# A graph network on one core: the compares of the source histogram cut into quarters

## The chip, the cores and the metric

The kernel runs on one core of a Trainium2 chip. The metric is the device time of one execution in microseconds (us). Three runs of the kernel before gave 4375.13, 4377.79 and 4395.61 us, a median of 4377.79 us.

## The reference

The reference computes two layers of a graph network over 12,500 nodes with 32 features and 212,500 edges (`src`, `dst`, sorted by `dst`). Cut to what matters here:

```python
h = relu(layernorm(x))
deg_out = segment_sum(ones, src); deg_in = segment_sum(ones, dst)
agg = segment_sum((h * rsqrt(max(deg_out, 1)))[src], dst)         # layer 1
x = x + relu((agg * rsqrt(max(deg_in, 1))) @ weight + bias)
h = relu(layernorm(x))
m = messages(h[src], edge_attr_4, relu(edge_attr_32 @ W1 + b1) @ W2 + b2)   # layer 2
x = x + segment_sum(m, dst) + skip(h)
```

`deg_out` is a histogram: how often each node stands in `src`.

## The kernel before, in words

The edges are cut into 208 chunks of 1024 (`CHUNKS`), a chunk into 8 tiles of 128 edges. Four chunks form a ring (`RING`): four buffers of the tile `g` hold the rows gathered for four chunks. The gather is on GpSimd (`POOL`, L352): one indirect DMA per tile of 128 edges, 8 to a chunk. It reads the row numbers in `idx`, which SyncE (`SP`) loads for each chunk after the gather that last used the slot has landed (`load1`, L286).

GpSimd's order is fixed. It first gathers rows of the input `x_rows` for the first 32 chunks (`EARLY`, 256 gathers, into a kept copy), since the normalised table isn't there yet. Then it waits for `table1_out` and gathers the 176 other chunks of layer 1 from `table1` (1408 gathers), then it waits for `table2_out` and gathers all 208 chunks of layer 2 from `table2` (1664 gathers).

`table1` needs the histogram of `src`, and the histogram is the part that the change touches. A node's number is split into two digits, `dig_p` (128 values, the partition) and `dig_r` (100 values, the row in it, `NR`), both bf16. For 16 tiles of 128 edges at a time (`HB` = 16, a batch; 104 batches in all, `HBATCH`), VectorE compares a constant with each digit, L749: one `is_equal` of 128 x 16 = 2048 elements a partition into `oh_p`, one of 100 x 16 = 1600 elements into `oh_r`. Both outputs and the constants are bf16. The second compare increments `hist_ready`. TensorE (L506 to L508) waits for it, multiplies the 16 one-hot pairs of the batch (`oh_p` as weights, `oh_r` as moving data, 100 columns) into one PSUM bank, and the last of the 16 increments `hist_used`. `oh_p` and `oh_r` have two buffers: before batch n VectorE waits until batch n - 2 was used (`wait(dve, hist_used, n - 1)`). After the last batch VectorE makes `norm_src` from the counts (L761 to L763) and the table `hn` (L764), and ScalarE's queue writes `table1` (L411). VectorE then goes on with the range of `dst` of every chunk (L769, L770), which SyncE writes out and reads back as `bound` (L298, L301) before it goes on with the `idx` of the first chunks that are gathered from `table1` (the second loop of `load1`).

Then VectorE clears the sums (L773, a memset) and starts on the segment sums of layer 1.

Of the kernel before, what the change touches and what calls it, by code (L numbers as in the profile page):

```python
# [26 lines left out]
ALU = mybir.AluOpType  # L27
# [6 lines left out]
P = 128  # L34
# [23 lines left out]
EPS = 1e-5  # L58
ALPHA, C110, SI_SCALE = 0.25, 1.0 / np.sqrt(3.0), 1.0 / np.sqrt(float(MUL))
HB = 16  # L60
HBATCH = CHUNKS * TILES // HB
EARLY_LINKS = 6
MID_LINKS = 24
# [3 lines left out]
def gnn_program(nc, x_rows, src_all, src_chunks, src_rows, dst_all, dst_chunks, edge_t, sh_chunks,  # L67
                w_l0, b_l0, w1, b1, w2, skip_w, sel_a, sel_b, ident_in, out):
    assert EARLY % RING == 0 and REG_ITERS > A_ITERS + 1
    assert CHUNKS % (2 * HB // TILES) == 0 and CHUNKS % 2 == 0  # L70
    with ExitStack() as ctx:
# [54 lines left out]
        dig_r, o = hist[:, o:o + T_ALL], o + T_ALL  # L126
        oh_p, o = hist[:, o:o + 2 * P * HB].rearrange("p (b j t) -> p b j t", b=2, t=HB), o + 2 * P * HB
        oh_r, o = hist[:, o:o + 2 * NR * HB].rearrange("p (b j t) -> p b j t", b=2, t=HB), o + 2 * NR * HB
        zero_b, o = hist[:, o:o + P], o + P
# [3 lines left out]
        iotas = prod_a[:, :, :, :].rearrange("p b t k -> p (b t k)").bitcast(BF16)  # L133
        iota_p = iotas[:, 0:P * HB].rearrange("p (j t) -> p j t", t=HB)
        iota_r = iotas[:, P * HB:(P + NR) * HB].rearrange("p (j t) -> p j t", t=HB)

# [68 lines left out]
        def wait(eng, s, value):  # L205

            if not isinstance(value, int) or value > 0:
                eng.wait_ge(s, value)
# [287 lines left out]
        def _(pe):  # L496
# [7 lines left out]
            def count(i):  # L504
                for b in range(2):
                    pe.wait_ge(hist_ready, 2 * i + b + 1)  # L506
                    for t in range(HB):
                        mm = pe.matmul(deg, oh_p[:, b, :, t], oh_r[:, b, :, t], start=False, stop=False,  # L508
                                       skip_group_check=True)
                    mm.then_inc(hist_used, 1)  # L510

            with pe.Fori(0, HBATCH // 2) as i:
                count(i)
# [157 lines left out]
        def _(dve):  # L671
# [72 lines left out]
            def count(i):  # L744
                for b in range(2):
                    n = 2 * i + b
                    wait(dve, hist_used, n - 1)
                    for iota, dig, oh, m in ((iota_p, dig_p, oh_p, P), (iota_r, dig_r, oh_r, NR)):
                        ins = dve.tensor_tensor(oh[:, b, :, :], iota,  # L749
                                                dig[:, None, bass.ds(n * HB, HB)].to_broadcast([P, m, HB]),  # L750
                                                ALU.is_equal)
                    ins.then_inc(hist_ready, 1)

            count(0)
            with dve.Fori(1, HBATCH // 2) as i:
                count(i)
# [389 lines left out]
```

## Time and profile before

| | us |
|---|---|
| median of 3 runs | 4377.79 |
| the profiled execution | 4373.49 |
| its span | 4371.7 |
| VectorE busy | 2761.8 (63%) |
| TensorE busy | 2969.1 (68%) |
| GpSimd busy | 3306.5 (76%) |

The span is cut into three stages: the histogram with its setup up to about 349 us, layer 1 up to about 2204 us (GpSimd's wait for the second table ends there), layer 2 after that. Busy time counts only what an engine executes: the 0.3 us between two gathers is not in GpSimd's 76%.

### The profile page before, as it was taken

How to read it: one execution, taken by the hardware profiler on the slowest of the kernel's cores; microseconds unless marked ns; L12 is line 12 of the kernel's file. 1: busy time of each engine (PE TensorE's matmuls, PEld its weight loads, DVE VectorE, ACT ScalarE, POOL GpSimd, SP SyncE). 2: the span in 40 equal slices, each digit the busy share in tenths (PEclk: the TensorE clock that was granted, in tenths of full speed). 3: DMA queues.
4: the chain of work that ended last, by engine and by line, in shares of the span. 5: the costliest groups of instructions: out<-in, count | busy, mean ns of one | idle time of the engine just before them, and what ended most of it. 6: DMA issues, size and time to landing. Idle time of an engine off the chain costs nothing.

```text
span 4371.7 us, 66218 instructions
## 1 busy us (share of the span) xinstructions
PE 2969.1 (68%) x17022; PEld 2223.1 (51%) x17023; DVE 2761.8 (63%) x4668; ACT 747.0 (17%) x2428; POOL 3306.5 (76%) x3334
## 2 busy tenths in 40 slices
PE   6993444444222222222279999999999999999999
PEld 5772444434222222211256667666666666666676
DVE  7775444343222222211169998999989999999898
ACT  0000000001000000000043333333323333333232
POOL 7777777777777777777767777777777777777775
PEclk9999965555555555555589998999999999999898
DMA  2002111111011011110111111111111111111111
GB/s 51 11 11 44 37 37 42 37 37 28 15 15 15 15 15 15 15 15 14 15 27 29 28 29 28 29 27 29 28 28 29 29 28 28 29 28 28 27 29 19
DMA packets 224085, 113.80 MB, mean 26 GB/s; under 512 B 148848, under 2 KB 212145, under 8 KB 223953
## 3 DMA queue, kind: packets, MB, share of 16 engines
q0 software_dynamic: 106496, 54.74, 8.5%
q1 hardware_dynamic: 106281, 39.22, 3.9%
q10 hardware_dynamic: 11280, 19.53, 1.3%
q8 instruction: 10, 0.16, 0.0%
q14 instruction: 18, 0.15, 0.0%
HBM read 108.30 MB, written 4.92 MB: 26 GB/s over the span
## 4 chain that ended last, share of the span: by engine, by line
POOL 62%; issue 23%; PE 7%; DVE 4%; DMA 2%; ACT 1%; POOLq 1%; DVEq 1%; ACTq 0%
POOL g L352 62%; PE ps L524 3%; PE ps L626 2%; DMA g<-table,idx 2%; PE ps L576 1%; PE ps L614 1%; DVE onehot L794 0%; ACT acc_b L454 0%; DVE hn L947 0%; DVE ef L930 0%; ACT root L425 0%; DVE stat L704 0%; DVE stat L701 0%; ACT q L475 0%; PE ps L660 0%
## 5 line engine op out<-in xcount | busy, mean ns | idle before, releaser
L352 POOL DMA_INDIRECT g<-table,idx x3072 | 2995.8, 975 | 955.7 <-issue 924.9
L524 PE MATMUL ps<-onehot,g 128*33 128x68 f32 x2816 | 350.4, 317 | 989.6 <-issue 954.6
L626 PE MATMUL ps<-w_s,hid 128*128 128x256 f32 x3328 | 901.3, 418 | 2.2 <-DVE prod_a L1002 2.0
L626 PEld LDWEIGHTS ps<-w_s,hid 128*128 128x128 f32 x3328 | 645.8, 204 | 452.7 <-issue 366.5
L524 PEld LDWEIGHTS ps<-onehot,g 128*33 128x33 f32 x2816 | 307.3, 173 | 1030.0 <-issue 1004.6
L1007 DVE TENSOR_REDUCE msg_b<-prod_b 128x128 f32<-128x1024 f32 x416 | 827.7, 1990 | 0.0
L806 DVE TENSOR_TENSOR acc_a<-acc_a,ps 33x68 f32 (+1 forms) x416 | 89.9, 216 | 1111.7 <-PE ps L524 1086.4
L614 PE MATMUL ps<-ef,w_s 32*64 32x512 f32 x832 | 479.9, 658 | 6.5 <-issue 6.4
L463 ACT ACTIVATE hid<-ps,b_s 64x512 f32<-64x512 f32 x416 | 282.2, 678 | 1153.2 <-PE ps L614 1151.1
L524 PEld LDWEIGHTS ps<-onehot,prod_a 128*128 128x128 f32 x3328 | 402.8, 194 | 121.8 <-issue 114.4
L524 PE MATMUL ps<-onehot,prod_a 128*128 128x68 f32 x3328 | 410.7, 277 | 76.7 <-issue 68.6
L475 ACT ACTIVATE q<-g,sh 128x32 f32<-128x32 f32 x1664 | 374.4, 308 | 298.3 <-DMA g<-table,idx 298.0
L991 DVE TENSOR_TENSOR prod_b<-ps,q 128x768 f32<-128x768 f32 x416 | 394.3, 948 | 18.4 <-PE ps L626 18.3
L352 POOL DMA_INDIRECT g<-x_rows,idx x256 | 310.1, 1211 | 79.8 <-issue 77.7
L794 DVE TENSOR_TENSOR onehot<-iota_all,dst_rel 128x544 f32<-128x544 f32 x416 | 299.6, 720 | 61.7 <-issue 53.2
L508 PE MATMUL ps<-acc_b 128*128 128x100 bf16 x1664 | 313.6, 370 | 33.5 <-DVE acc_b L749 33.5
L508 PEld LDWEIGHTS ps<-acc_b 128*128 128x128 bf16 x1664 | 246.5, 148 | 100.4 <-DVE acc_b L749 33.6
L1002 DVE TENSOR_TENSOR prod_a<-ps,q 128x512 f32<-128x512 f32 x416 | 283.0, 680 | 0.0
L524 PE MATMUL ps<-onehot,msg_b 128*56 128x68 f32 x3328 | 250.0, 231 | 0.0
L524 PEld LDWEIGHTS ps<-onehot,msg_b 128*56 128x56 f32 x3328 | 218.4, 134 | 15.1
L425 ACT ACTIVATE root<-stat 128x4 f32<-128x4 f32 x50 | 10.3, 205 | 1092.4 <-DVEq L698 1092.4
L976 DVE TENSOR_TENSOR vsh<-g,sh 128x192 f32<-128x192 f32 x208 | 80.7, 388 | 166.0 <-ACT q L476 165.1
(111 smaller groups left out, 1936.3 us busy)
## 6 DMA issues: line engine op xcount, KB each, us to landing
g<-table,idx POOLq DMA_INDIRECT x3072
ef<-edge_t SPq DMA_DIRECT2D x208, 128.0 KB
ef<-src_rows ACTq DMA_DIRECT2D x31, 512.0 KB, 3.6
idx<-src_chunks SPq DMA_DIRECT2D x416, 4.0 KB
g<-x_rows,idx POOLq DMA_INDIRECT x256
sh<-sh_chunks SPq DMA_DIRECT2D x208, 16.0 KB
table<-hn ACTq DMA_DIRECT2D x1, 1600.0 KB, 8.4
table<-hn ACTq DMA_DIRECT2D x25, 64.0 KB, 1.6
```

The lines of the kernel that those rows point to most:

```text
L352: pool.indirect_dma_start(out=g[:, j, t, 0:FEAT], out_offset=None, in_=table, in_offset=bass.IndirectOffsetOnAxis(ap=idx[:, j, t:t + 1], a ...
L463: act.activation(hid[0:HID, h, :], ps[0:HID, H_BANK + h, :], ACT.Relu, bias=b1_s[:, 0:1]).then_inc(hidden_ready, 1)
L475: act.activation(q[:, j % 2, t, 8:40], g[:, j, t, 0:FEAT], ACT.Copy, scale=sh[:, j, t, 0:1])
L508: mm = pe.matmul(deg, oh_p[:, b, :, t], oh_r[:, b, :, t], start=False, stop=False, skip_group_check=True)
L524: mm = pe.matmul(ps[0:m, S_BANK + b, col:col + WIN], r, oh(t), start=(t == 0), stop=(t == TILES - 1))
L614: pe.matmul(ps[0:HID, H_BANK + h, :], w1_s[32 * j:32 * j + 32, :], ef[32 * j:32 * j + 32, 512 * h:512 * h + 512], start=True, stop=True, t ...
L626: mm = pe.matmul(w_ps[h][:, t, :], hid[:, h, P * t:P * t + P], w2_s[:, :], start=True, stop=True)
L794: dve.tensor_tensor(onehot[:, b, :, :], iota_all[:, None, 0:WIN].to_broadcast([P, TILES, WIN]), dst_rel[:, bass.ds(c * TILES, TILES)][:, : ...
L806: ins = dve.tensor_tensor(here, here, ps[0:m, S_BANK + b, col:col + WIN], ALU.add)
L991: dve.tensor_tensor(prod_b[:, h, :, 0:3, :].rearrange("p t m (i o) -> p t m i o", o=MUL), w[:, :, 128:192].rearrange("p t (i o) -> p t i o ...
L1002: dve.tensor_tensor(prod_a[:, b, 4 * h:4 * h + 4, :].rearrange("p t (k o) -> p t k o", o=MUL), w[:, :, 0:128].rearrange("p t (k o) -> p t ...
L1007: dve.tensor_reduce(msg_b[:, b, 4 * h:4 * h + 4, 0:32].rearrange("p t (g o) -> p t g o", o=MUL), prod_b[:, h, :, :, :].rearrange("p t g (i ...
```

## The change

Each of the two compares of a batch becomes four. The output and the constant are cut along the digit's values: four times 32 x 16 = 512 elements in place of 2048, and four times 25 x 16 = 400 in place of 1600. The digits (`dig`) are the same 16 columns for each piece. `hist_ready` is incremented by the last of the eight, and the wait for `hist_used` still stands ahead of the first. Nothing else is changed.

```diff
+PIECES = 4
 ...
                     n = 2 * i + b
                     wait(dve, hist_used, n - 1)
                     for iota, dig, oh, m in ((iota_p, dig_p, oh_p, P), (iota_r, dig_r, oh_r, NR)):
-                        ins = dve.tensor_tensor(oh[:, b, :, :], iota,
-                                                dig[:, None, bass.ds(n * HB, HB)].to_broadcast([P, m, HB]),
-                                                ALU.is_equal)
+                        for part_m in range(0, m, m // PIECES):
+                            rows_m = slice(part_m, part_m + m // PIECES)
+                            ins = dve.tensor_tensor(oh[:, b, rows_m, :], iota[:, rows_m, :],
+                                                    dig[:, None, bass.ds(n * HB, HB)].to_broadcast([P, m // PIECES, HB]),
+                                                    ALU.is_equal)
                     ins.then_inc(hist_ready, 1)
```

## Rows read from the trace of the kernel before

**Rows 1.** The page: the chain that ended last, and GpSimd's two gather groups.

```profile
POOL 62%; issue 23%; PE 7%; DVE 4%; DMA 2%; ACT 1%; POOLq 1%; DVEq 1%; ACTq 0%
...
L352 POOL DMA_INDIRECT g<-table,idx x3072 | 2995.8, 975 | 955.7 <-issue 924.9
...
L352 POOL DMA_INDIRECT g<-x_rows,idx x256 | 310.1, 1211 | 79.8 <-issue 77.7
```

**Rows 2.** The longest wait of GpSimd: us in total, times, longest.

```profile
POOL g L352 <- DMA table<-hn: 19.9, 1, 19.9
```

**Rows 3.** Line L749, the compares: duration in ns min/median/max, first and last start; then the idle time before them.

```profile
L749 DVE TENSOR_TENSOR acc_b<-prod_a,msg_b x104: 1220/1226/1230, 33.3 to 343.2; 128x2048 bf16<-128x2048 bf16 x104
...
L749 DVEq FUSED_REGOPS  x102: 65/69/82, 38.7 to 343.1; - x102
...
  PE ps L508: 90.9, 102
```

**Rows 4.** Timeline, VectorE and TensorE at the first three batches: start us, duration us.

```profile
34.45 0.98 DVE L749 TENSOR_TENSOR acc_b<-prod_a,acc_b 128x1600 bf16<-128x1600 bf16 x1
35.35 1.22 DVE L749 TENSOR_TENSOR acc_b<-prod_a,msg_b 128x2048 bf16<-128x2048 bf16 x1
35.49 0.58 PE L508 MATMUL ps<-acc_b 128*128 128x100 bf16 x2 [33.48 <-DVE acc_b L749]
38.86 1.23 DVE L749 TENSOR_TENSOR acc_b<-prod_a,msg_b 128x2048 bf16<-128x2048 bf16 x1 [1.39 <-PE ps L508]
```

**Rows 5.** Timeline 101 to 104 us, VectorE and GpSimd, one period of the histogram.

```profile
101.49 0.94 POOL L352 DMA_INDIRECT g<-x_rows,idx  x1 [0.30 <-issue]
102.17 1.23 DVE L749 TENSOR_TENSOR acc_b<-prod_a,msg_b 128x2048 bf16<-128x2048 bf16 x1 [0.90 <-PE ps L508]
102.74 1.47 POOL L352 DMA_INDIRECT g<-x_rows,idx  x1 [0.30 <-issue]
103.31 0.98 DVE L749 TENSOR_TENSOR acc_b<-prod_a,acc_b 128x1600 bf16<-128x1600 bf16 x1
```

**Rows 6.** Timeline 353 to 392 us, GpSimd and VectorE, after the histogram.

```profile
353.08 3.43 POOL L352 DMA_INDIRECT g<-x_rows,idx  x1 [0.30 <-issue]
355.61 2.28 DVE L769 TENSOR_REDUCE mm_c<-prod_b 104x2 f32<-104x2048 int32 x1
...
363.76 10.78 DVE L773 MEMSET acc_a<- 128x12868 f32 x1 [2.75 <-issue]
364.62 0.94 POOL L352 DMA_INDIRECT g<-x_rows,idx  x1 [0.30 <-issue]
365.87 0.94 POOL L352 DMA_INDIRECT g<-x_rows,idx  x1 [0.30 <-issue]
...
391.45 0.94 POOL L352 DMA_INDIRECT g<-table,idx  x1 [0.30 <-issue]
```

**Rows 7.** Timeline 355 to 373 us, the DMA queues of ScalarE and SyncE.

```profile
355.72 0.45 ACTq L411 DMA_DIRECT2D table<-hn  x1
...
366.24 6.22 SPq L286 DMA_DIRECT2D idx<-src_chunks  x2
```

**Rows 8.** DMA issues of the same stretch: KB each, median us to landing.

```profile
table<-hn ACTq DMA_DIRECT2D x1, 1600.0 KB, 8.4
bound<-bounds SPq DMA_DIRECT2D x2, 104.0 KB, 4.6
```

**Rows 9.** Timeline 2405 to 2407 us, short VectorE instructions in layer 2.

```profile
2405.26 0.94 DVE L991 TENSOR_TENSOR prod_b<-ps,q 128x768 f32<-128x768 f32 x1
2406.13 0.41 DVE L996 TENSOR_TENSOR prod_b<-ps,q 128x256 f32<-128x256 f32 x1
2406.46 0.68 DVE L1002 TENSOR_TENSOR prod_a<-ps,q 128x512 f32<-128x512 f32 x1
2407.06 1.99 DVE L1007 TENSOR_REDUCE msg_b<-prod_b 128x128 f32<-128x1024 f32 x1
```

## Prediction, made before the changed kernel was run

> **What bounds the kernel.** I read the chain of waits first. 62% of it is GpSimd's gathers and 23% is "issue", the 0.3 us between two of them [rows 1]. GpSimd has one large wait, 19.9 us for a table [rows 2]. It is the one for the second table, at the end of layer 1, because the first gather from table 1 at 391.45 us stands 0.30 us behind the gather before it, like any other [rows 6]. So the histogram isn't waited for. It could end later, up to a point, at no cost, and an earlier end brings nothing. What counts in the first 391 us is how fast GpSimd gets through its 256 gathers from the input.
>
> Those are slow: 1211 ns each against 975 ns later [rows 1]. Undisturbed, a gather takes 0.94 us and the next starts 1.25 us later (364.62, 365.87 [rows 6]). In the histogram they alternate between 0.94 and 1.47 us [rows 5]. The long ones tell why. The one at 102.74 ends at 104.21, 0.90 us after VectorE's second compare starts at 103.31 [rows 5]; the one at 353.08 ends at 356.51, 0.90 us after VectorE goes on to L769 at 355.61 [rows 6]. So about 0.05 us into a gather GpSimd needs something that a running compare holds; it gets it at the end of that one instruction, even if VectorE goes on at once, and needs 0.90 us from there. VectorE's memset of 10.78 us, under which gathers take 0.94 us [rows 6], doesn't hold it. The Trainium skill says of this (SBUF — State Buffer, "Who interferes with whom") that a VectorE instruction with two SBUF inputs contends with a GpSimd instruction that reads SBUF. The trace agrees, but not with its "whole instruction" the other way round: no compare is longer than 1230 ns, with 104 of them beside gathers [rows 3].
>
> The histogram itself is set by TensorE. From 38.86 to 343.2 us there are 101 batches, 3.01 us each, and before 102 of them VectorE waits for TensorE, 0.89 us on average [rows 3, 4]. Two gathers fit into a batch: 2 x 1.25 + 0.51 of waiting = 3.01.
>
> **The change, part by part.**
>
> *VectorE's time.* Removed: 208 compares; added: 832. What one costs beside the streaming is to be read from start to start, since a compare without a wait starts some 0.08 us before the record of the last ends: 1.14 us for 2048 elements (102.17, 103.31 [rows 5]), 0.90 for 1600 (34.45, 35.35 [rows 4]). In layer 2, 256, 512 and 768 f32 elements take 0.33, 0.60 and 0.87 us: 1.05 ns an element and 0.06 us fixed [rows 9]. Half of 1.05 ns (bf16) for 2048 and 1600 leaves 0.07 us fixed. I take 0.07, the row nearest in kind. A piece of 512 then takes 0.27 + 0.07 = 0.34, one of 400 takes 0.21 + 0.07 = 0.28, the eight 2.48 us in place of 2.04. Lower bound of the fixed part: the straight line through 1.14 and 0.90 gives 0.04 (eight: 2.3). Upper bound: the records' whole durations, no overlap, 0.16 (eight: 3.15).
>
> *Does the histogram get longer?* TensorE starts on batch 1 at 35.49 + 3.01 = 38.50 and VectorE on batch 2 at 38.86, 0.36 later. The first matmul stands 0.06 us behind the end of the last compare (35.43 [rows 4]). A batch is ready in time if 0.36 + body + 0.08 + 0.06 is at most 3.01. Before: 0.50 + 2.04 = 2.54, 0.47 to spare. After: 2.98, 0.03 to spare. So the period stays 3.01 us, barely. Beyond that the loop through both engines sets it, (3.01 + 0.50 + body) / 2. Only the first batch's extra 0.44 us moves the end.
>
> *GpSimd.* Here a gain could be expected: a gather now waits for a piece of at most 0.34 us, not for 1.14. But I walk it through, with times from a batch's first compare. The pieces end at 0.34, 0.68, 1.02, 1.36, 1.64, 1.92, 2.20, 2.48, free time follows up to 3.01, and a request comes 1.25 after the last grant (0.90 + 0.30 + 0.05). Granted at 2.48, the next request comes at 3.73, which is 0.72 of the next batch, in the third piece: granted at 1.02. The next at 2.27, in the last piece: granted at 2.48. That closes: two gathers a batch, as before. The neighbouring cycle (0.68, 1.93 to 2.20, 3.45 = 0.44 to 0.68) closes too, and a grant in the free time, say at 2.70, comes to 0.94, is granted at 1.02 and falls in. The waits are shorter and there are more of them, and their sum is again 0.51 us a batch. So GpSimd's rate stays 1.51 us and nothing is gained.
>
> *After the histogram.* All of it moves by 0.4 us at most. The long gather at 353.08 lost 2.5 us [rows 6]; another phase may meet L764 and what follows differently, which is +-3 us.
>
> Sum against the profiled execution: 4373.49 + 0 +- 3. The median of the runs is 4.3 us above it; I carry that: 4378 us.
>
> **The rivals.**
>
> *A: the lock opens.* If the fixed part is 0.05 or below (the straight line above gives 0.04), the pieces end at 0.32, 0.63, 0.95, 1.27, 1.53, 1.78, 2.04, 2.30, and the walk goes 2.30, 0.63, 2.04, 0.32, 1.78, 0.02 (free), 1.27, 2.52 (free), 0.95 and 2.30: nine gathers in four batches, 1.34 us each. Over 312 us that is 232 gathers where there were 206, 33 us ahead, and ahead of stalls such as that at 353.08. GpSimd would be done with the input at about 355 us. Then it waits, since the table lands at 355.72 + 8.4 = 364.1, and its first `idx` is issued at 366.24, behind `bound` [rows 7, 8]. With bound's 4.6 us less a little, it lands at about 370.3. So the gain is cut at 391.45 - 370.4 = 21, less the 0.4: 4353 profiled, 4357 as a median. Against it: 0.06 to 0.07 from rows 4, 5 and 9. For it: the margins of the lock are small (0.72 against a piece that starts at 0.68), and any other small gap between pieces would open it too. Partly open, it gives anything from 0 to 20.
>
> *B: VectorE becomes the bound.* With 0.16 us fixed, body 3.15, the period is (3.51 + 3.15) / 2 = 3.33, the histogram ends 33 us later, and the `idx` chain puts GpSimd's first table gather at 370.4 + 33 = 403.7, 12 us behind 391.45: 4390 as a median. It decides from 3.21 us a batch (21 us / 104 more than 3.01), body 2.9. The sequencer's address step, 0.07 us once a batch [rows 3], could come four times and add to it. Against it: short instructions overlap in rows 9. The Trainium skill speaks for it (VectorE: DVE Perf Modes, "The DRAIN you can't avoid": the next op doesn't start until the pipe is empty, and the errata section lets every small tile pay its latency, "(N+151)/0.96"). By that formula the eight would be an estimated 3.16 us. The starts in rows 4, 0.08 us ahead of the ends, don't agree.
>
> *C: starvation.* If GpSimd is served only when VectorE really pauses, and not between two short compares, it is granted once a batch, at 2.48 (a request at 0.72 waits through). Then it does 104 gathers in the histogram where it did 206, and the missing 102 follow at 1.25: 128 us more, 4506. It decides as soon as the boundary between two pieces is too short for a grant. Against it: the boundary at 103.31, with no pause either, gave a grant [rows 5]; such boundaries are more frequent now, not shorter. The same sign would come from pieces that run at the f32 rate of rows 9 (body 4.4, period 3.95, the histogram 98 us later, 77 of it beyond the slack of 21); nothing speaks for it, since the innermost 16 elements stay as they are.
>
> **How the numbers follow.** No change (4371 to 4384): 0.57. A in full: 0.27, in part: 0.05. B: 0.07. C and its like: 0.04. The likeliest is no change, 4378. Cases of both signs stand beside it, so the wide range is 4352 to 4391: A's median with its spread below, B's above. A measurement of this kernel tells about 0.5%, 22 us, from no change. A's 21 us lies just under that: counted as faster in a good third of its cases, 0.12. Slower by 22 us is C and the worst of B: 0.05. Within: 0.83.
>
> **What would show it.** Right: 832 compares with starts 0.34 and 0.28 us apart, batches of 3.01 us, VectorE's wait before a batch down from 0.89 to about 0.45, gathers from the input still 1.21 us on average but of two kinds near 1.15 and 1.25, and the first table gather at 391 us. A: gathers at 1.34 us apart and then one wait of GpSimd up to 370 us. B: no waits of VectorE for L508, a period over 3.1. C: gathers of 2.5 us and more. I am wrong if the first table gather moves by more than 4 us, or if layers 1 and 2 behind it don't merely move along with it.

## The result, and the profile after

The changed kernel takes 4357.58 us (median of 7 runs, 4353.97 to 4360.65) where the kernel before takes 4376.69 in the same series. The ratio is 0.9955, interval 0.9943 to 0.9966: 19 us or 0.45% faster. The forecast of no change (4378) was wrong; the time is that of rival A (4357), which had been given 0.27 and had set the lower end of the stated range, 4352 to 4391. The profiled execution took 4357.06 us, its span is 4355.2.

The page and the waits of GpSimd, of the changed kernel (line numbers are 1 to 3 higher: L353 is the gather, L509 the histogram's matmul, L752 the compares, L287 the load of `idx`):

```profile
POOL 54%; issue 21%; PE 15%; DVE 5%; DMA 2%; ACT 1%; DVEq 1%; POOLq 0%; SPq 0%; ACTq 0%
...
L353 POOL DMA_INDIRECT g<-table,idx x3072 | 2999.4, 976 | 969.4 <-issue 923.6
...
L353 POOL DMA_INDIRECT g<-x_rows,idx x256 | 276.6, 1080 | 79.8 <-issue 77.7
```

```profile
POOL g L353 <- DMA table<-hn: 19.7, 1, 19.7
POOL g L353 <- DMA idx<-src_chunks: 16.8, 4, 14.1
```

Against [rows 1] the gathers from the input fell from 1211 to 1080 ns and those from the tables did not move. Against [rows 2] there is a new wait of 14.1 us, for `idx`. And TensorE's share of the chain rose from 7 to 15%: in the first 371 us the chain now runs through the histogram. The compares, with the columns of [rows 3], and the wait ahead of a batch:

```profile
L752 DVE TENSOR_TENSOR acc_b<-prod_a,msg_b x416: 413/419/471, 33.3 to 345.1; 128x512 bf16<-128x512 bf16 x139
L752 DVE TENSOR_TENSOR acc_b<-prod_a,acc_b x416: 351/359/380, 34.6 to 346.3; 128x400 bf16<-128x400 bf16 x139
...
  PE ps L509: 48.9, 102
```

All 832 are there. A batch takes 3.02 us on average where it took 3.01, and TensorE's last product of the histogram ends at 350.0 us where it ended at 349.1, so the histogram is 0.9 us longer than before. What answers to [rows 6] and [rows 7]:

```profile
354.12 3.41 POOL L353 DMA_INDIRECT g<-x_rows,idx  x1 [0.30 <-issue]
356.64 2.28 DVE L772 TENSOR_REDUCE mm_c<-prod_b 104x2 f32<-104x2048 int32 x1
356.75 0.45 ACTq L412 DMA_DIRECT2D table<-hn  x1
...
367.26 1.93 SPq L287 DMA_DIRECT2D idx<-src_chunks  x4
371.63 0.94 POOL L353 DMA_INDIRECT g<-table,idx  x1 [14.10 <-DMA idx<-src_chunks]
```

GpSimd issues its last gather from the input at 354.12 us, where it was 390.2: 36 us ahead. It then stands for 14.1 us, and the first gather from the table comes at 371.63 in place of 391.45. So 19.8 us are gained there. Of the 16 us that are lost, 13.8 go into the wait (14.1 in place of the usual 0.3) and 2.5 into the last gather, which VectorE's long instruction at L767 holds. At the last gather of the kernel the lead is 16.5 us; the layers in between took it up and down between 12.0 and 22.4 us.

A view of one window shows the rate: its start and end, its length, GpSimd's busy time in it with the number of gathers, then the clock granted to TensorE, the DMA share and GB/s. GpSimd's gathers from 50 to 330 us, before and after:

```profile
50.00:330.00 280.00, 223.35 (x186) 1.00 0.08 11
```

```profile
50.00:330.00 280.00, 216.39 (x209) 1.00 0.10 15
```

280 / 186 is 1.51 us a gather, 280 / 209 is 1.34.

### The profile page after: what moved, and what is told of

Same layout as the page of the kernel before. It is cut to its first block, busy times and chain, and to the rows that moved or that the text cites. A ratio compares the mean times of both kernels' runs of the same rounds, so it can differ in the third digit from the quotient of the medians.

```text
span 4355.2 us, 66842 instructions
## 1 busy us (share of the span) xinstructions
PE 2975.1 (68%) x17022; PEld 2218.5 (51%) x17023; DVE 2807.7 (64%) x5292; ACT 747.2 (17%) x2428; POOL 3276.5 (75%) x3334
## 4 chain that ended last, share of the span: by engine, by line
POOL 54%; issue 21%; PE 15%; DVE 5%; DMA 2%; ACT 1%; DVEq 1%; POOLq 0%; SPq 0%; ACTq 0%
POOL g L353 54%; PE ps L509 7%; PE ps L525 3%; DMA g<-table,idx 2%; PE ps L627 2%; PE ps L577 1%; PE ps L615 1%; DVE onehot L797 1%; ACT q L476 0%; ACT acc_b L455 0%; DVE prod_b L994 0%; PE ps L661 0%; DVE hn L950 0%; PE ps L663 0%; DVE xc L714 0%
## 5 line engine op out<-in xcount | busy, mean ns | idle before, releaser
L353 POOL DMA_INDIRECT g<-table,idx x3072 | 2999.4, 976 | 969.4 <-issue 923.6
L509 PE MATMUL ps<-acc_b 128*128 128x100 bf16 x1664 | 314.1, 370 | 33.9 <-DVE acc_b L752 33.9
L353 POOL DMA_INDIRECT g<-x_rows,idx x256 | 276.6, 1080 | 79.8 <-issue 77.7
L509 PEld LDWEIGHTS ps<-acc_b 128*128 128x128 bf16 x1664 | 240.2, 148 | 107.5 <-DVE acc_b L752 38.9
```

The source lines that it names most:

```text
L353: pool.indirect_dma_start(out=g[:, j, t, 0:FEAT], out_offset=None, in_=table, in_offset=bass.IndirectOffsetOnAxis(ap=idx[:, j, t:t + 1], a ...
```

## The experiments

Two theories stood against each other after the result. **Lock** (a closed cycle of requests and grants): a gather asks for something 0.05 us after its start; it is let through if no compare runs or the running one has only just begun (0.07 us), else at that compare's end; 1.25 us later comes the next request. Whether gathers gain then depends on where the pieces end, not on how long they are on average. **Mean wait:** shorter compares make for shorter waits, in proportion to the sum of squared lengths.

**Halves, and the first compare only.** `PIECES = 2`; and four pieces for `oh_p`, one for `oh_r`.

> Both compares in two pieces (1024 and 800 elements) in place of four. Theory 1 (lock: a gather is granted at the end of the compare it finds running, or at once if that compare started less than 0.07 us ago or none runs; 1.25 us later comes the next request): the pieces end at 0.60, 1.20, 1.69, 2.18 of a batch of 3.01 us. The walk closes at two gathers a batch (e.g. granted at 1.69, the next request at 2.94, free, then 1.17, granted at 1.20, 2.45 free, 0.69, granted at 1.20, 2.45 free, and so on), so gathers stay 1.51 us apart, the first table gather stays at 391 us and the time is that of the kernel before, 4376 us within 4. Theory 2 (no lock, shorter pieces help in proportion: the mean wait is the sum of squared piece lengths over twice the period, 0.20 us): gathers 1.45 us apart, nine more in the histogram, some 11 us gained, 4365 us.

> Only the first compare in four pieces, the second whole. Theory 1 (lock): pieces end at 0.34, 0.67, 1.01, 1.34, then 2.24. A request in the second compare goes to 2.24, the next comes at 0.48 and goes to 0.67, the next at 1.92 and goes to 2.24: two a batch, 1.51 us apart, no change, 4376 us within 4. Theory 2 (in proportion): mean wait 0.21 us, gathers 1.46 us apart, some 10 us gained, 4366 us. If half of the change is enough for all of its gain (4357), both are wrong.

Measured: halves 4372.51 us against 4372.44 before, ratio 0.9996 (0.9986 to 1.0006), gathers 1.51 us apart, first table gather at 390.3. First compare only: 4371.99, ratio 1.0003 (0.9993 to 1.0013), 1.51 us, 390.3. Both came out as the lock theory has it and not by mean wait. GpSimd's window in each (halves, then first only):

```profile
50.00:330.00 280.00, 223.34 (x186) 1.00 0.09 11
```

```profile
50.00:330.00 280.00, 223.32 (x187) 1.00 0.09 11
```

**The order of the pieces.** These two runs decide. Five pieces a batch in two orders; the work, the number and the lengths are the same.

```diff
-for iota, dig, oh, m in ((iota_p, dig_p, oh_p, P), (iota_r, dig_r, oh_r, NR)):
+for iota, dig, oh, cuts in ((iota_p, dig_p, oh_p, (49, 45, 34)), (iota_r, dig_r, oh_r, (49, 51))):   # open
+for iota, dig, oh, cuts in ((iota_p, dig_p, oh_p, (34, 49, 45)), (iota_r, dig_r, oh_r, (49, 51))):   # closed
```

> Five pieces a batch (ten compares in a turn of the loop): 49, 45 and 34 of the 128 values, 49 and 51 of the 100; they end at 0.48, 0.92, 1.27, 1.75 and 2.25 us of the batch. Lock theory with 0.07 us let through at the start of a piece: granted at 2.25, the next request comes at 0.48 of the next batch, as the second piece has just begun, and is let through; then 1.73 goes to 1.75, 3.00 is free, 1.24 goes to 1.27, 2.52 is free, 0.76 goes to 0.92, 2.17 goes to 2.25, and again: seven gathers in three batches, 1.29 us apart, GpSimd done with the input at about 345 us, the first table gather set by what lies behind the histogram at 371 us: 0.45% faster than before where before takes 4370. Without the 0.07 us, 0.48 goes to 0.92, 2.17 to 2.25: closed, 1.51 us. Mean wait theory: 0.17 us, 1.42 us apart, the same for both of these kernels.

> The same five pieces, only the 34 values first: 34, 49, 45 and 49, 51, ending at 0.35, 0.83, 1.27, 1.75 and 2.25 us. Lock theory: granted at 2.25, the next request at 0.48 falls into the second piece, 0.13 after its start, and goes to 0.83; the next at 2.08 goes to 2.25: closed, two gathers a batch, 1.51 us apart, first table gather at 390 us, no faster than before. Mean wait theory: 1.42 us, as the other kernel. On a chip where before takes some 6010 us: the same distances, if ten compares a turn don't bring the standstills of sixteen.

Measured on one chip: 34 last, 4353.56 us, ratio to before 0.9956 (0.9942 to 0.9970); 34 first, 4370.58 us, ratio 0.9985 (0.9973 to 0.9998), 3.6 us faster than before where no gain was expected. GpSimd's windows, 34 last and 34 first:

```profile
50.00:330.00 280.00, 213.93 (x217) 1.00 0.11 15
```

```profile
50.00:330.00 280.00, 223.50 (x186) 1.00 0.09 11
```

1.29 and 1.51 us, to the digit what the lock theory said, and 17 us between two kernels that differ in the order of five compares. The first table gather stands at 370.7 and 391.0 us (first start in each row):

```profile
L353 POOL DMA_INDIRECT g<-table,idx x3072: 938/944/2108, 370.7 to 4316.9; - x192
L353 POOL DMA_INDIRECT g<-table,idx x3072: 940/944/2167, 391.0 to 4340.2; - x192
```

Mean wait is out. The timelines show the deciding gather, first with 34 last, then with 34 first (the compares stand on L754 there):

```profile
204.80 0.57 DVE L754 TENSOR_TENSOR acc_b<-prod_a,msg_b 128x784 bf16<-128x784 bf16 x1 [0.70 <-PE ps L509]
205.23 0.96 POOL L353 DMA_INDIRECT g<-x_rows,idx  x1 [0.30 <-issue]
205.28 0.53 DVE L754 TENSOR_TENSOR acc_b<-prod_a,msg_b 128x720 bf16<-128x720 bf16 x1
```

```profile
202.43 0.56 DVE L754 TENSOR_TENSOR acc_b<-prod_a,msg_b 128x784 bf16<-128x784 bf16 x1
202.53 1.28 POOL L353 DMA_INDIRECT g<-x_rows,idx  x1 [0.30 <-issue]
202.90 0.53 DVE L754 TENSOR_TENSOR acc_b<-prod_a,msg_b 128x720 bf16<-128x720 bf16 x1
```

In the first the request (205.28) meets the boundary between two pieces and the gather takes 0.96 us. In the second it comes 0.15 us after a piece began, waits for 202.90 and ends 0.91 us after that.

**A writer that reads nothing.** The compares are replaced by memsets of the same parts; the histogram's counts are left out by it.

```diff
-ins = dve.tensor_tensor(oh[:, b, rows_m, :], iota[:, rows_m, :], dig[...].to_broadcast([P, m // PIECES, HB]), ALU.is_equal)
+ins = dve.memset(oh[:, b, rows_m, :], 1.0)
```

> Leaves out the compares: each of the eight pieces is a memset of the same part of the same output, so the degrees are wrong constants. A memset reads nothing. If the two-input compare is what holds the gathers up, none of the gathers beside the histogram is longer than 0.95 us, they stand 1.25 us apart, and GpSimd is done with the input about 20 us earlier than in the changed kernel, yet the first table gather stays within 1 us of 371 us, since the histogram is TensorE's and the transfers behind it are unchanged: 4357 us within 5. If any VectorE write into the tile slows the gathers, they stay at 1.34 us.

Measured: 4447.74 us, ratio 1.0168 (1.0147 to 1.0190, two runs). The expectation of the time and of the first table gather was wrong, that of the gathers beside the histogram right. Gathers and memsets:

```profile
L353 POOL DMA_INDIRECT g<-x_rows,idx x225: 940/944/953, 49.4 to 329.0; - x113
```

```profile
L752 DVE MEMSET acc_b<- x832: 392/438/485, 33.5 to 434.3; 128x400 bf16 x84, 128x512 bf16 x83
```

No gather takes over 0.953 us, so writing the one-hot tiles holds nothing up; what holds a gather comes with the compare, which also reads. Reading alone isn't enough either. In the layers of the kernel before, 394 gathers ask while VectorE multiplies `prod_b<-ps,q`, with one of its two inputs in PSUM, and 681 while it reduces `msg_b<-prod_b`, with one input: none of them takes over 0.961 us. Both inputs of a compare are in SBUF. But the memsets stand 0.54 and 0.42 us apart, which is slower than the compares (0.34 and 0.28), a batch takes 3.86 us, and the histogram ends at 438 us. GpSimd's first table gather then comes at 459 us after a wait of 127.9. That is 68 us later than in the kernel before, and the kernel is 75 us slower. So this is rival B's mechanism, a histogram that VectorE limits and that GpSimd then waits for, seen at work with another price.

**The cap.** SyncE loads the row numbers for the first table gathers ahead of the bounds.

```diff
-            with sp.Fori(0, EARLY_ITERS - 1) as i:
+            with sp.Fori(0, EARLY_ITERS) as i:
                 load1(i)
 ...
-            with sp.Fori(EARLY_ITERS - 1, ITERS - 1) as i:
+            with sp.Fori(EARLY_ITERS, ITERS - 1) as i:
                 load1(i)
```

> The changed kernel, and SyncE loads the row numbers of the first chunks that are gathered from the table before it handles the chunks' bounds, not after. If the gain of the change is cut by the row numbers' transfer behind the bounds (GpSimd starts on the table at 371.6 us, the table landed at about 365.2), GpSimd now starts at about 365.4: 6 us more gained, 4351 us. If the cut is the table itself or something else, nothing moves: 4357.

Measured: 4353.74 us against 4372.44, ratio 0.9948 (0.9931 to 0.9964). The wait changed its cause, as expected:

```profile
364.95 0.95 POOL L353 DMA_INDIRECT g<-table,idx  x1 [13.21 <-DMA table<-hn]
```

6.7 us were won at that point. Whether they reach the end isn't settled. In this execution the second table's first gather stands at 2184.2 us and at 2183.2 in the changed kernel, so layer 1 took them back; the ratios 0.9948 and 0.9955 come from separate series and their intervals overlap.

**The same kernels on other chips.** The changed kernel and three variants ran beside the kernel before on one chip and again on a second, and some of them on a third. On these three chips the kernel before takes 5856 to 6016 us instead of 4375.

> The changed kernel once more, to stand on one chip beside the kernels below. 0.5% faster than before, the first table gather at 371.6 us.

> The kernel with the row numbers loaded ahead of the bounds once more, now beside the changed kernel. If its start on the table 6.7 us earlier is kept to the end, it is 6 to 7 us (0.15%) faster than the changed kernel. If the segment sums of layer 1 take it back (the first look had the second table at the same time in both), the two are the same within 2 us.

> Eight pieces as in the changed kernel, but cut unevenly: 31, 37, 28 and 32 of the 128 values, 15, 29, 35 and 21 of the 100. VectorE's work, the number of pieces and their mean length are those of the changed kernel. Theory 1 (lock with the 0.07 us at the start of a piece in which a gather is let through): the pieces end at 0.33, 0.70, 1.01, 1.34, 1.54, 1.85, 2.21 and 2.45. Granted at 2.45, the next request comes at 0.69 of the next batch, goes to 0.70, the next at 1.95, 0.11 after the start of the piece 1.85 to 2.21 and so too late, goes to 2.21, the next at 0.45 goes to 0.70 again: closed, two gathers a batch, 1.51 us apart, the first table gather at about 390 us, the time of the kernel before. Theory 2 (mean wait by squared lengths: 0.13 us as against 0.125): gathers 1.34 to 1.38 us apart, 371.6 us, the time of the changed kernel.

> The first compare in eight pieces of 256 elements, the second in five of 320: thirteen pieces, at 0.07 us fixed each a body of 2.79 us. The loop through both engines gives (3.51 + 2.79) / 2 = 3.15 us a batch in place of 3.01 and the histogram ends 13 to 15 us later than in the changed kernel. Gathers are freer still (1.26 to 1.31 us apart; without the 0.07 us at the start of a piece 1.34), but GpSimd waits for the table: the first table gather at 385 us, 6 to 7 us ahead of the kernel before, 4370 against 4376. If a short piece costs 0.16 us instead, the body is 3.96, the period 3.7 and the kernel is 1% slower than before.

> The uneven cut again (31, 37, 28, 32 and 15, 29, 35, 21 rows), on a chip on which the kernel before takes some 4370 us. Theory 1 (lock with 0.07 us let through at the start of a piece): closed at grants 0.70 and 2.21, gathers 1.51 us apart, first table gather at about 390 us, the time of the kernel before. Theory 2 (mean wait): gathers 1.34 to 1.38 us apart, first table gather at 371.6 us, 0.4% faster than before.

> The changed kernel beside the others on one chip: 0.4% to 0.5% faster than before, first table gather at 371.6 us.

> The row numbers ahead of the bounds, beside the changed kernel: first table gather at 365 us. If the 6.7 us are kept, 0.15% faster than the changed kernel; if the gathers' luck in the layers takes them back, the same within 2 us.

> Thirteen pieces (eight of 256, five of 320 elements). At 0.07 us fixed each the body is 2.79 us, the loop through both engines gives 3.13 to 3.15 us a batch, the histogram ends 13 to 15 us later than in the changed kernel, the first table gather comes at 385 us: 4370 where before is 4376. If a piece costs 0.16 us, the period is 3.7 and the kernel 1% slower than before. Gathers 1.26 to 1.31 us apart if a gather is let through in the first 0.07 us of a piece, 1.34 if not.

> The kernel before, unchanged, for its trace. If the chip is one on which it takes some 6010 us: the changed kernel's histogram ends at 648 us there since VectorE stands for 42 to 43 us in nine turns of its loop while GpSimd gathers. If the longer loop body is the cause, this trace has no such standstill in the histogram, which ends near 349 us, and that 299 us is the whole difference of the two kernels there. If the standstill has nothing to do with the body, it is here too. On a chip with some 4370 us: as the first profile, gathers 1.51 us apart.

> The uneven cut. Where VectorE doesn't stand still: theory 1 (lock, 0.07 us let through at the start of a piece) has gathers 1.51 us apart and the first table gather at about 390 us, the time of before; theory 2 (mean wait) has 1.34 to 1.38 us, 371.6 us, 0.4% faster. On the other kind of chip it is as the changed kernel, 4.8% slower, and tells nothing of the two.

> The uneven cut. Where VectorE doesn't stand still: lock theory 1.51 us between gathers and the first table gather at 390 us; mean wait theory 1.34 to 1.38 us and 371.6 us. On a chip where before takes some 6010 us: 4.8% slower, as before.

> Two pieces of each compare, eight compares in a turn of the loop (four in the kernel before, sixteen in the changed one). On a chip where before takes some 6010 us: if the standstills in the histogram come with any body longer than before's, the histogram ends near 650 us; if eight still pass, it ends at 349 us and the kernel is as before. On a chip with some 4370 us: no change, as in its first run.

| kernel | us, ratio to before there (interval) | last matmul of the histogram starts at us |
|---|---|---|
| changed, first chip | 6302.00, 1.0498 (1.0475 to 1.0521) | 648.3 |
| changed, second chip | 6295.79, 1.0484 (1.0456 to 1.0511) | 647.7 |
| idx early, the same two | 6289.41, 1.0479 and 6292.60, 1.0459 | 648.1 and 646.5 |
| uneven eight pieces, first chip twice, second, third | 6313.66, 6304.92, 6290.50, 6197.22: 1.0509, 1.0481, 1.0472, 1.0581 | 644 to 648 |
| thirteen pieces, first and second chip | 6308.62 (four runs, 6236.81 to 6347.87), 1.0523 and 6272.51, 1.0456 | 600.7 and 596.7 |
| before, one run, first chip | 6038.02 (6015.64 beside it) | 348.7 |
| halves, third chip | 5886.85 in the profiled run, 6118.83 in the other, beside 5856.47 | 348.8 in the profiled run |

There the change is 4.8 to 5% slower, and on the first two chips the histogram accounts for it: it ends 299 us later (648 against 349), the first table gather comes 278.5 us later, and the whole kernel is 293 and 284 us slower. The uneven cut on the third chip is 341 us slower with the same histogram; what the rest of that is stays open. VectorE in the changed kernel on the second chip:

```profile
82.08 1.43 DVE L752 TENSOR_TENSOR acc_b<-prod_a,msg_b 128x512 bf16<-128x512 bf16 x4 [28.45 <-remote]
83.43 1.21 DVE L752 TENSOR_TENSOR acc_b<-prod_a,acc_b 128x400 bf16<-128x400 bf16 x4
126.87 1.43 DVE L752 TENSOR_TENSOR acc_b<-prod_a,msg_b 128x512 bf16<-128x512 bf16 x4 [42.23 <-remote]
128.22 1.19 DVE L752 TENSOR_TENSOR acc_b<-prod_a,acc_b 128x400 bf16<-128x400 bf16 x4
```

One batch, then 42 us in which VectorE does nothing. From 53 us on there are eight such stops, six of them 40 to 43 us long; GpSimd's last gather from the input starts at 342.4 us, the last stop ends at 371 us, and from then on a batch takes 3.02 us. "remote" is what the profile writes where it finds no releaser. The profiled run of the kernel before has none of it on such a chip: its histogram runs at 3.01 us a batch and its gathers at 1.51, as in [rows 5]. A turn of VectorE's loop is two batches: with four and eight compares in a turn (before, halves) the one trace of each from these chips has no stop, with sixteen and twenty-six all ten traces from these chips have them. The other run of the halves took 232 us longer than the traced one and has no trace, so whether eight compares always pass isn't known. Nor does length alone order it: with sixteen compares the first stop comes after five or six batches, with twenty-six after 29 or 30. The cause is open. The loading of the loop's code, held up by the gathers' traffic, is a guess that no run tried. The early idx is 12.6 and 3.2 us ahead of the changed kernel beside it, in runs that spread over 17 to 63 us, so its worth stays open. The uneven cut was meant to tell lock from mean wait and tells nothing here, since VectorE hardly runs while GpSimd gathers; the two orders of five pieces took its place. Of the thirteen pieces one number stands: after the stops a batch takes 3.16 us, where 3.13 to 3.15 was expected from a body of 2.79. The starts of its pieces stand 0.202 us (256 elements) and 0.235 us (320) apart, so short compares do cost 0.07 us each and no more.

## Why the prediction was wrong

**Price of a piece: right.** 0.34 and 0.28 us from start to start were forecast; the trace has 0.336 and 0.277. VectorE's wait ahead of a batch fell from 0.89 to 48.9 / 102 = 0.48 us (0.45 forecast), and the period went from 3.01 to 3.02 us on average, where only some hundredths of a us were to spare.

**What holds a gather: right for the compares, except at a compare's very start (next step).** It is 0.90 us from the end of the compare to the end of the gather, at every length of compare that was run. One gather of the kernel before, after the histogram, doesn't fit and stays unexplained: it starts 0.26 us after the reduction of L770 and ends 0.81 us after the cast that follows it, so it waited through both.

```profile
357.80 2.27 DVE L770 TENSOR_REDUCE mm_c<-prod_b 104x2 f32<-104x2048 int32 x1
358.06 3.76 POOL L352 DMA_INDIRECT g<-x_rows,idx  x1 [0.30 <-issue]
360.00 1.02 DVE L772 CAST dst_rel<-acc_a 128x1664 f32<-128x1664 int32 x1
```

**The walk through a batch: this step failed.** It let a request wait whenever a piece was running, so it took "(0.68, 1.93 to 2.20, 3.45 = 0.44 to 0.68)" for a closed cycle, kept GpSimd at 1.51 us a gather and put the gain at nothing. The runs showed that a request in the first 0.07 us of a piece isn't held: 1.34 us a gather, and 19.8 us gained at the first table gather. The trace of the changed kernel, one batch that starts at 205.21:

```profile
204.36 1.15 POOL L353 DMA_INDIRECT g<-x_rows,idx  x1 [0.30 <-issue]
205.21 0.42 DVE L752 TENSOR_TENSOR acc_b<-prod_a,msg_b 128x512 bf16<-128x512 bf16 x1 [0.51 <-PE ps L509]
205.82 0.97 POOL L353 DMA_INDIRECT g<-x_rows,idx  x1 [0.30 <-issue]
205.88 0.42 DVE L752 TENSOR_TENSOR acc_b<-prod_a,msg_b 128x512 bf16<-128x512 bf16 x1
207.09 0.94 POOL L353 DMA_INDIRECT g<-x_rows,idx  x1 [0.30 <-issue]
207.11 0.38 DVE L752 TENSOR_TENSOR acc_b<-prod_a,acc_b 128x400 bf16<-128x400 bf16 x1
208.33 1.10 POOL L353 DMA_INDIRECT g<-x_rows,idx  x1 [0.30 <-issue]
```

The gather of 205.82 asks at 205.87, is let through at 205.88 as a piece ends (0.67 of the batch: the cycle's first station), and the next asks at 207.14 or 1.93, as forecast. But the piece that is running had begun at 207.11, 0.03 before, and the gather isn't held: 0.94 us. It doesn't go to 2.20, and the cycle opens. The forecast's first cycle (0.72 to 1.02, 2.27 to 2.48) opens in the same way on its own numbers: 0.72 is 0.04 after the start of a piece. In the trace the batches also alternate between 3.00 and 3.04 us on average, so that after a grant at 2.46 one request came at 0.66, just ahead of the boundary at 0.67, and another at 0.68, just behind it and not held. I had named that margin as small and given the step more trust than it had. The distances then repeat every four batches with nine gathers, 1.34 us each.

All the gathers of the histogram settle where the edge lies. In the changed kernel's trace 39 of them ask within 0.065 us of the start of a piece, and none is held; 140 ask 0.077 us or more after it while it runs, and all are held to its end. Replaying the rule on the recorded starts of the compares from 50 to 330 us separates the edge from the jitter: without the 0.07 us it gives 187 gathers, with it 209, and the trace has 209. For the five pieces with 34 last it is 205 and 217, and the trace has 217; in that kernel the jitter would have opened the cycle in part. In the kernel before both give 186, so its histogram doesn't show the miss. But the trace of before had it elsewhere, in rows that I passed over: a gather that starts 0.01 us after a two-input instruction of 1.93 us isn't held, and the next one, 1.26 us into the same instruction, is.

```profile
374.60 1.93 DVE L776 TENSOR_TENSOR dst_rel<-dst_rel,bound 128x1664 f32<-128x1664 f32 x1
374.61 0.95 POOL L352 DMA_INDIRECT g<-x_rows,idx  x1 [0.30 <-issue]
375.86 1.49 POOL L352 DMA_INDIRECT g<-x_rows,idx  x1 [0.30 <-issue]
```

**Rival A: right in its size, by luck in part.** It asked for a cost of 0.05 us or less for each piece, and that cost is 0.07. Its walk also breaks the forecast's own rule: the request at 0.02 is called free, but the first piece of the batch had just begun there. Held to 0.32, it would go on to 1.57, be granted at 1.78 and come back to 0.02, two gathers a batch. So its nine gathers in four batches come from the edge that the forecast had left out, not from shorter pieces. Its cut at the `idx` chain (370.4 forecast, 371.6 measured) and its 33 us of lead (36 measured) hold, and the run with the early `idx` confirms that the cut is the `idx` transfer and then the table.

**Rivals B and C.** C, starvation, is excluded: each boundary between two pieces grants. B didn't decide: short compares overlap, 0.336 and 0.277 us from start to start with records of 0.42 and 0.36. Its mechanism showed with memsets. That a turn of the loop could cost far more by its length, as on the other chips, was in no rival.

**"All of it moves along": nearly.** Of 19.8 us at the first table gather 16.5 arrive at the end of the profiled execution and 19 in the medians.

The five pieces with 34 last reach the change's gain on 520 compares in place of 832, with ten in a turn. That kernel was not run on a chip of the other kind.

## What to carry to other kernels

Where two engines exclude each other and both run in a loop, look for a cycle: the average wait says little, and the sum of the waits is whatever fills up the common period. The order and the cuts of the instructions can open or close it at no cost in work. Before such a walk is trusted, allow for the edges of every instruction and for the period's jitter; a closed cycle whose margins are 0.01 to 0.04 us of a 3 us period is no firm forecast and should be given the chance of one that isn't. The rule of the walk can be tested first: replay it on the recorded starts, and look in the trace for a request near an edge.

Check what an engine's lead is worth before counting it: of 36 us won on GpSimd, 13.8 were waited away for a small transfer that stands behind an unrelated one in a queue.

## What the runs showed of the hardware

- A gather is held by a compare only if it asks between some 0.07 us after the compare's start (0.065 passed, 0.077 didn't, in the changed kernel's trace) and its end. The one let through costs the compare little: the piece of 400 at 207.11 takes 0.38 us in place of 0.36. By the Trainium skill (SBUF — State Buffer, "SBUF: two separate sides") whichever starts first gets the shared ports for the whole instruction and the other blocks. For a gather that comes first that doesn't hold here: the compare at 102.17 starts 0.68 us into a gather of 0.94 us and takes its usual 1.23 us [rows 5].
- A bf16 memset of 512 elements takes 0.54 us from start to start, longer than a two-input compare of as many (0.34).
- On three of the five chips of these experiments a VectorE loop of 16 compares a turn stood for some 42 us a batch while GpSimd gathered; the one trace each of 4 and of 8 compares a turn from these chips has no such stop. The same change cost 5% there and gained 0.45% on a chip of the other kind.
